# Attention in a fused attention and mixture-of-experts layer: V products cut in two round a maximum product, and the transpose of the maxima placed between the halves

## The chip, the cores and the metric

The kernel runs on one core of one Trainium2 chip. The metric is the device time of one execution, in microseconds (us). Engines named here: PE (TensorE, matrix products; "PEld" is its loading of weights), DVE (VectorE), ACT (ScalarE), POOL (GpSimd) and SP, which issues most DMAs.

## The reference, cut to what matters

Two sequences of 512 tokens with 512 features pass a layer norm, attention with 32 heads of 16 features, a second layer norm and a mixture of 8 experts (2 per token). The change lies in the attention alone:

```python
q, k, v = (proj(w_q), proj(w_k), proj(w_v))            # (2, 32, 512, 16)
scores = jnp.einsum('bhqd,bhkd->bhqk', q, k) / jnp.sqrt(jnp.float32(D_K))
attn = jax.nn.softmax(scores, axis=-1)
out = jnp.einsum('bhqk,bhkd->bhqd', attn, v)
```

## The kernel before, in words

The 64 pairs of sequence and head are worked on in NG = 16 groups of four heads. Softmax needs each query's maximum before the exponentials, and the kernel computes the scores twice. First with queries on the partitions: 16 **maximum products** a group (`key_max`, L759: 48 rows, 128 queries, 512 keys), each followed on DVE by a maximum over its 512 keys (`maximum`, L1466) that ends as one column of neg_max. When all 16 columns of a group are there, PE transposes neg_max (`max_t`, L750), ACT copies the result to max_rows (`maxima`, L1201), and SP sends it by DMA as a 49th row into the stacks q_stack (L486). Then with keys on the partitions: eight **score units** a group of two products each (`scores`, L771), where the 49th row subtracts the maximum; ACT takes the exponential of each unit (L1251) into probs_t. The **V product** (`pv`, L740) multiplies probs_t (128 keys by 512 queries) with v_ones, for four heads at once: each head uses a strip of 32 columns of the array (`tile_position=(0, 32*j)`) and writes 32 partitions of the bank ps_o. Its operands are plain fp32, and each call becomes two matmul records. Four V products, one per 128 keys, make a group; then ACT copies ps_o to o_raw (L1236).

The main loop on PE, `for a, b in steps` (L875 to L904), runs over **quarters**, four to a group. A quarter has four maximum products of the group two ahead (called K0 to K3 here), one V product (V), and two score units (S and S'). Its order before is K0, K1, V, K2, [T], S, K3, S', where T is the transpose of the maxima, in one quarter of four (a % 4 = 1). In the quarters a = 1 to 28 of the loop the number b of the score side is the same as a; after a = 28 one quarter has no maximum products, and from then on b = a + 1. The last quarters, b = 57 and later, have no maximum products either.

Maximum products and transposes take turns in a ring of three PSUM banks (`max_banks`, L361; `turns`, L337 to L343). A turn may start when the reader of the turn three before has finished (`max_bank_free`, L428): DVE's maximum (s_mx), or, where that turn was a transpose, ACT's copy (s_mr). The table of turns and the order of the loop have to agree.

K0 and K2 use rows 0 to 47 of the array, K1 and K3 rows 64 to 111, and the two products of a score unit one half each, so two of these products can be in the array together. All engines execute in the order of the program. ACT's order in a quarter is: the copy o_raw (where b % 4 = 1; it waits for all V products of the group), the copy max_rows (in a transpose quarter), and two exponentials. DVE's is its four maxima, plus a reciprocal (L1529) and a shuffle (L1544) once in two groups.

Of the kernel before, what the change touches and what calls it, by code (L numbers as in the profile page):

```python
# [5 lines left out]
B, S, HID = 2, 512, 512  # L6
# [3 lines left out]
TPB = S // P  # L10
# [6 lines left out]
NG = B * NH // GH  # L17
UNITS = 8
# [27 lines left out]
def moe_layer(nc: bass.Bass, x, wq, wk, wv, wo, gw, w13, w2, w2t, out):  # L46
# [8 lines left out]
    with ctx:  # L55
        def sem(name):
            return ctx.enter_context(nc.semaphore(name))

        def sb(c, name, shape, dt=f32):
            return c.enter_context(nc.sbuf_tensor(name, shape, dt))  # L60
# [41 lines left out]
        q0 = sb(att, "q_stack0", q_shape, f32r)  # L102
# [8 lines left out]
        q1 = sb(att, "q_stack1", q_shape, f32r)  # L111
# [11 lines left out]
        probs_t = sb(att, "probs_t", [P, 2, GH, S])  # L123
# [96 lines left out]
        ps_o = ctx.enter_context(nc.psum_tensor("ps_o", [P, 512], f32))  # L220
# [22 lines left out]
        s_ja = sem("s_ja")  # L243
# [9 lines left out]
        s_ex = sem("s_ex")  # L253
        s_pv = sem("s_pv")
        s_or = sem("s_or")
# [47 lines left out]
        a_count = [n + 1 for n in range(len(jobs))]  # L303
# [20 lines left out]
        def head_at(g, j, rows):  # L324

            at, slot, row = (g // 2) % RING, 2 * (g % 2) + j // 2, HALF * (j % 2)
            return [t[at][row:row + rows, slot, :] for t in (qs, ks)]

        def scores_at(u2):

            pair, par = divmod(u2, 2)
            slot, qt = divmod(pair, TPB)
            return 2 * slot + par, qt, par * 2 * TPB + slot * TPB + qt
# [2 lines left out]

        turns = []  # L337
        for s in range(-2, NG):
            lead = 2 if s < 0 else 7
            turns += [(s + 2, u2) for u2 in range(lead)]  # L340
            turns += [(s + 1, "maxima")] * (s + 1 >= 0)
            turns += [(s + 2, u2) for u2 in range(lead, 4 * TPB)]
        turns = [t for t in turns if t[0] < NG]  # L343

        steps, b = [], 0
# [8 lines left out]
        def group_done(a, b):  # L354

            if a is not None and a % TPB == 1:
                return a // TPB + 1
            return NG - 1 if b == TPB * (NG - 2) + 1 else None
# [66 lines left out]
        def max_bank(g, what):  # L425
            return max_banks[turn_of[g, what] % 3]

        def max_bank_free(eng, g, what):  # L428

            n = turn_of[g, what] - 3  # L430
            if n >= 0:
                before, what = turns[n]
                if what in ("maxima", "projection", "router"):
                    eng.wait_ge({"maxima": s_mr, "projection": s_res, "router": s_t2e}[what], before + 1)
                else:
                    eng.wait_ge(s_mx, before * 16 + what + 1)
# [288 lines left out]
        def _(pe):  # L725
            def three(o, x_hi, x_lo, w_hi, w_lo, start, stop):

                pe.matmul(o, x_hi, w_hi, start=start, stop=False)  # L728
                pe.matmul(o, x_hi, w_lo, start=False, stop=False)  # L729
                return pe.matmul(o, x_lo, w_hi, start=False, stop=stop)  # L730

            def pv(g, kc):

                if not 0 <= g < NG:
                    return
                pe.wait_ge(s_ex, UNITS * g + 2 * (kc + 1))
                if kc == 0 and g >= 1:
                    pe.wait_ge(s_or, g)
                for j in range(GH):
                    last = pe.matmul(ps_o[32 * j:32 * j + 32, :],  # L740
                                     v_ones[:, (g // 8) * TPB + kc, (g % 8) * GH + j, :, :].rearrange("p d o -> p (d o)"),
                                     probs_t[:, kc % 2, j, :], start=(kc == 0), stop=(kc == TPB - 1),
                                     tile_position=(0, 32 * j))
                last.then_inc(s_pv, 1)

            def max_t(g):

                pe.wait_ge(s_mx, 16 * (g + 1))
                max_bank_free(pe, g, "maxima")
                pe.transpose(max_bank(g, "maxima")[0:4 * GH, 0:P], neg_max[:, g % 2, :], ident[:, :]).then_inc(s_mt, 1)  # L750

            def key_max(g, u2):

                if g >= NG:
                    return
                j, qt, _ = scores_at(u2)
                q, k = head_at(g, j, ROWS)
                max_bank_free(pe, g, u2)
                pe.matmul(max_bank(g, u2), q[:, qt * P:(qt + 1) * P], k, start=True, stop=True).then_inc(s_sn, 1)  # L759
# [19 lines left out]
            def opened(o, at, b, i):  # L779

                wide, x2 = (w_hi[0], w_lo[0]), (xnT_hi, xnT_lo)
                pe.wait_ge(s_ja, a_count[n_of[("t", b, TPB - 1)]])
                if i:
                    pe.wait_ge(s_wh, 1)
                else:
                    pe.wait_ge(s_wqh, 1)
                terms = ((0, 0), (0, 1), (1, 0)) if i else ((0, 0), (1, 0), (0, 1))
                for n, (wp, xp) in enumerate(terms):
                    if xp:
                        pe.wait_ge(s_jd, d_count[n_of[("t", b, TPB - 1)]])  # L790
                    elif wp and i:
                        pe.wait_ge(s_wl, 1)
                    elif wp:
                        pe.wait_ge(s_wql, 1)
                    for c in range(HC):
                        last = pe.matmul(o, wide[wp][:, c, at], x2[xp][:, c, :], start=(n == c == 0),  # L796
                                         stop=(n == 2 and c == HC - 1))
                return last

            def v_tail(o, i, c0, c1):  # L800

                at = slice(i * P, (i + 1) * P)
                for c in range(c0, c1):
                    last = three(o, xnT_hi[:, c, at], xnT_lo[:, c, at], w_hi[2][:, c, :], w_lo[2][:, c, :],
                                 c == 0, c == HC - 1)
                return last

            for n, (kind, b, i) in enumerate(jobs[:-1]):
# [10 lines left out]
                if kind == "t":  # L819
                    pe.wait_ge(s_xn, b * TPB + i + 1)  # L820
                    for c in range(HC):
                        last = pe.transpose(o[:, c * P:(c + 1) * P], x_sb[:, b * TPB + i, c * P:(c + 1) * P], ident[:, :])
                else:
# [3 lines left out]
                    if opening:  # L827
                        last = opened(o, at, b, i)
# [3 lines left out]
                    for c in range(0 if opening else HC):  # L832
                        x2 = [t[:, c, :] for t in (xnT_hi, xnT_lo)]
                        w2 = [t[which][:, c, :] for t in (w_hi, w_lo)]
                        if kind == "v":
                            last = three(o, *(t[:, at] for t in x2), *w2, c == 0, c == HC - 1)
                        else:
                            last = three(o, *(t[:, at] for t in w2), *x2, c == 0, c == HC - 1)
# [36 lines left out]
            for a, b in steps:  # L875
                ga, pa = (NG, 0) if a is None else (2 + a // TPB, a % TPB)
                s, p = divmod(b, TPB)
                group, kc = (s - 1, p + 2) if p < 2 else (s, p - 2)
                done = group_done(a, b)
                if ga < NG and pa == 0 and ga % 2 == 0:  # L880
                    pe.wait_ge(s_stack[(ga // 2) % RING], 16 * 12 * (ga // 2 // RING + 1))
                if p == 0 and s < NG:
                    pe.wait_ge(s_row[s % 4], 32 * (s // 4 + 1))

                if b == 0:
                    pe.wait_ge(s_ja, a_count[n_of["v", 1, TPB - 3]])
                    v_tail(ps_o[:, :], TPB - 1, 0, HC // 2)
                key_max(ga, 4 * pa)
                key_max(ga, 4 * pa + 1)
                if b == 0:  # L890
                    pe.wait_ge(s_ja, a_count[n_of["v", 1, TPB - 2]])
                if b == 1:
                    v_tail(ps_o[:, :], TPB - 1, HC // 2, HC).then_inc(s_job, 1)
                if (group, kc) == (0, 0):
                    pe.wait_ge(s_ja, a_count[-1])
                pv(group, kc)
                key_max(ga, 4 * pa + 2)
                if done is not None:
                    max_t(done)
                scores(s, 2 * p)  # L900
                key_max(ga, 4 * pa + 3)
                scores(s, 2 * p + 1)
                if b in FILL:
                    projection(*FILL[b])  # L904
# [70 lines left out]
            for d in range(1, NT):  # L975
                pe.matmul(ps_m[:, d * E:NT * E], ones_b[:, :], pk[:, 0:(NT - d) * E],
                          start=(d == 1), stop=False, skip_group_check=True)
            pe.matmul(ps_m[:, 0:NT * E], before_b[:, :], pk, start=False, stop=True,
                      skip_group_check=True).then_inc(s_rank_0, 1)
            for t in range(NT):  # L980
                last = pe.matmul(ps2[:, 0, 0:E], ones_b[:, :], pk[:, t * E:(t + 1) * E],
                                 start=(t == 0), stop=(t == NT - 1))
# [5 lines left out]
            for t in range(NT):  # L988
                last = pe.matmul(ps4[:, 0, 0:2], row_hot_0[:, t, :], token_of_0[:, t, :],
                                 start=(t == 0), stop=(t == NT - 1))  # L990
# [176 lines left out]
            for half, done in enumerate((s_xt_0, s_xt)):  # L1167
                for c in range(2):
                    at = slice((2 * half + c) * P, (2 * half + c + 1) * P)
                    last = pe.transpose(ps2[:, half, c * P:(c + 1) * P], xg[:, 1, at], ident[:, :])  # L1170
# [696 lines left out]
```

## Time and profile before

| | us |
|---|---|
| median of 3 runs (562.98 to 564.12) | 563.24 |
| the profiled execution | 562.15 |
| its span, which the trace covers | 560.3 |
| PE busy | 537.7 (96%) |
| DVE busy | 386.5 (69%) |
| ACT busy | 324.6 (58%) |

The attention loop takes the stretch from about 95 to 267 us. A busy PE is not PE at its peak: the ends of matmuls are modelled, and of two products in the array together both count. The time at the start of a row is from the start of the span; in brackets stands how long the engine was idle before the row and what released it.

### The profile page before, as it was taken

The page shows a single profiled execution, that of the slowest core. Times are in us where ns is not written, and L with a number is a line of the kernel's source. Part 1 is how long each engine was busy: PE and PEld are TensorE (multiplying, and loading weights), DVE is VectorE, ACT ScalarE, POOL GpSimd, SP SyncE. Part 2 cuts the span into 40 slices and gives each one's busy share as a digit, 9 for nine tenths or more (in the row PEclk, how much of TensorE's full clock was granted, in tenths as well). Part 3 has the DMA queues.
Part 4 walks back from the last instruction along what each step waited for, and adds up shares of the span by engine and source line. Part 5 has one row for each costly group of instructions (what it writes and reads, how often), then busy time and mean ns, then how long its engine had stood idle before and what let it go on. Part 6 is the DMA issues. An engine that isn't in the chain of part 4 may idle for free.

```text
span 560.3 us, 9693 instructions
## 1 busy us (share of the span) xinstructions
PE 537.7 (96%) x3504; PEld 391.4 (70%) x3504; DVE 386.5 (69%) x706; ACT 324.6 (58%) x480; POOL 116.2 (21%) x145
## 2 busy tenths in 40 slices
PE   8999999899999999999999989999999999999991
PEld 6887665333333333333778979999999999999980
DVE  6914657889998999961688986755728375667650
ACT  4322115767878777878345463746657475757540
POOL 3400111002022020622001203234341321241212
PEclk9999999999999999999998999999999999999996
DMA  8390368937465753004464599583764757586112
GB/s 329 103 112 2 56 83 98 114 47 89 70 97 76 92 75 99 12 19 165 156 223 134 185 352 329 145 309 51 287 153 154 267 144 278 117 299 160 32 30 37
DMA packets 29068, 78.19 MB, mean 140 GB/s; under 512 B 7644, under 2 KB 8924, under 8 KB 24538
## 3 DMA queue, kind: packets, MB, share of 16 engines
q1 hardware_dynamic: 23722, 68.84, 47.0%
q0 software_dynamic: 5296, 8.69, 8.4%
q8 instruction: 30, 0.49, 0.4%
q14 instruction: 20, 0.16, 0.1%
HBM read 53.11 MB, written 9.32 MB: 111 GB/s over the span
## 4 chain that ended last, share of the span: by engine, by line
PE 77%; DVE 13%; issue 3%; DMA 2%; ACT 2%; POOL 1%; SPq 0%; POOLq 0%; DVEq 0%; ACTq 0%
PE ps L728 15%; PE ps L729 14%; PE ps L730 14%; PE ps_o L740 8%; DVE neg_max L1466 8%; PE ps L759 6%; PE ps L771 4%; PE ps_m L759 3%; PE ps L796 2%; DVE w_lo L1575 1%; DMA w_sb<-w 1%; PE ps L777 1%; PE ps_o L728 1%; PE ps_m L728 1%; PE ps_m L1022 1%
## 5 line engine op out<-in xcount | busy, mean ns | idle before, releaser
L1251 ACT ACTIVATE probs_t<-ps 128x1024 f32<-128x1024 f32 x128 | 124.2, 1022 | 32.9 <-PE ps L771 32.3
L1466 DVE TENSOR_REDUCE neg_max<-ps 128x1 f32<-128x512 f32 x170 | 111.8, 685 | 14.7 <-PE ps L759 12.1
L728 PE MATMUL ps<-xgT_hi,w_hi 128*128 128x256 f32 (+7 forms) x380 | 109.5, 288 | 1.0 <-DVE xgT_lo L1732 1.0
L729 PE MATMUL ps<-xgT_lo,w_hi 128*128 128x256 f32 (+7 forms) x380 | 108.5, 286 | 0.0
L730 PE MATMUL ps<-xgT_hi,w_lo 128*128 128x256 f32 (+7 forms) x380 | 108.5, 286 | 0.0
L759 PE MATMUL ps<-k_stack,q_stack 48*128 48x512 f32 x170 | 70.3, 456 | 3.8 <-issue 1.7
L728 PEld LDWEIGHTS ps<-xgT_hi,w_hi 128*128 128x128 f32 x380 | 72.0, 189 | 1.3 <-DVE xgT_lo L1732 1.1
L729 PEld LDWEIGHTS ps<-xgT_lo,w_hi 128*128 128x128 f32 x380 | 72.0, 189 | 0.1
L730 PEld LDWEIGHTS ps<-xgT_hi,w_lo 128*128 128x128 f32 x380 | 71.9, 189 | 0.0
L740 PE MATMUL ps_o<-probs_t,v_ones 128*32 128x512 f32 x512 | 68.1, 605 | 0.0
L1749 DVE TENSOR_TENSOR act<-gate,ps 128x256 f32<-128x256 f32 (+7 forms) x48 | 20.7, 430 | 67.8 <-PE ps L730 53.5
L759 PEld LDWEIGHTS ps<-k_stack,q_stack 48*128 48x128 f32 x170 | 28.3, 184 | 52.2 <-DVE neg_max L1466 43.0
L771 PE MATMUL ps<-q_stack,k_stack 49*128 49x512 f32 x256 | 62.1, 430 | 0.4 <-ACT probs_t L1251 0.4
L1466 DVE TENSOR_REDUCE neg_max<-ps_m 128x1 f32<-128x512 f32 x86 | 58.9, 684 | 3.0 <-PE ps_m L759 2.8
L1575 DVE TENSOR_TENSOR w_lo<-w_sb,w_hi 128x1024 fp32r<-128x1024 f32 x48 | 56.5, 1219 | 0.0
L1324 ACT ACTIVATE gate<-ps 128x256 f32<-128x256 f32 (+7 forms) x48 | 18.8, 393 | 61.6 <-PE ps L730 60.4
L1273 ACT ACTIVATE w_hi<-w_sb 128x1024 fp32r<-128x1024 f32 x48 | 48.6, 1056 | 4.2 <-DMA w_sb<-w 4.0
L759 PE MATMUL ps_m<-k_stack,q_stack 48*128 48x512 f32 x86 | 39.3, 457 | 1.0 <-DMA q_stack<-max_rows 0.2
L771 PEld LDWEIGHTS ps<-q_stack,k_stack 49*128 49x128 f32 x256 | 30.1, 185 | 12.3 <-ACT probs_t L1251 7.7
L646 POOL TENSOR_TENSOR q_hi<-q_hi,rec_all 128x512 f32<-128x512 f32 x7 | 9.0, 1284 | 136.1 <-DVE rec_all L1544 136.1
L688 POOL DMA_INDIRECT out<-xn,to_now x20 | 33.8, 1688 | 6.2 <-issue 6.2
L759 PEld LDWEIGHTS ps_m<-k_stack,q_stack 48*128 48x128 f32 x86 | 15.8, 184 | 25.5 <-DVE neg_max L1466 22.5
(329 smaller groups left out, 982.2 us busy)
## 6 DMA issues: line engine op xcount, KB each, us to landing
w_sb<-w SPq DMA_DIRECT2D x16, 1024.0 KB
w_sb<-w SPq DMA_DIRECT2D x8, 1536.0 KB
w_sb<-w SPq DMA_DIRECT2D x8, 1152.0 KB
q_stack<-q_hi SPq DMA_DIRECT2D x32, 128.0 KB, 5.4
k_stack<-k_hi SPq DMA_DIRECT2D x32, 128.0 KB, 5.1
q_stack<-q_lo SPq DMA_DIRECT2D x16, 128.0 KB, 4.7
k_stack<-k_lo SPq DMA_DIRECT2D x16, 128.0 KB, 5.9
q_hi<-o_raw SPq DMA_DIRECT2D x16, 128.0 KB, 4.7
```

What stands on the lines that cost most here:

```text
L688: pool.indirect_dma_start(out=out[:, :], out_offset=bass.IndirectOffsetOnAxis(ap=to_now[0:rows, m:m + 1], axis=0), in_=y_sb[0:rows, m, :], ...
L728: pe.matmul(o, x_hi, w_hi, start=start, stop=False)
L729: pe.matmul(o, x_hi, w_lo, start=False, stop=False)
L730: return pe.matmul(o, x_lo, w_hi, start=False, stop=stop)
L740: last = pe.matmul(ps_o[32 * j:32 * j + 32, :], v_ones[:, (g // 8) * TPB + kc, (g % 8) * GH + j, :, :].rearrange("p d o -> p (d o)"), prob ...
L759: pe.matmul(max_bank(g, u2), q[:, qt * P:(qt + 1) * P], k, start=True, stop=True).then_inc(s_sn, 1)
L771: last = pe.matmul(ps4[:, 2 * (n % 2) + c, :], k[:, kc * P:(kc + 1) * P], q, start=True, stop=True)
L1251: a.activation(probs_t[:, kc % 2, 2 * half:2 * half + 2, :], ps4[:, 2 * (n % 2):2 * (n % 2) + 2, :], ACT.Exp, scale=D ** -0.5).then_inc(s_ ...
L1273: a.activation(w13_hi[:, at], w13_sb[:, at], ACT.Copy).then_inc(s_hi13, 1)
L1466: v.tensor_reduce(neg_max[:, g % 2, col:col + 1], max_bank(g, u2), AX.X, ALU.max, negate=True).then_inc(s_mx, 1)
L1575: v.tensor_tensor(w13_lo[:, at], w13_sb[:, at], w13_hi[:, at].bitcast(f32), ALU.subtract).then_inc(s_lo13, 1)
L1749: v.tensor_tensor(act[:, u % 2, 0:cap], gate[:, u % 2, 0:cap], ps4[:, pair + 1, 0:cap], ALU.mult).then_inc(s_act, 1)
```

## The change

1. V is issued in two halves: queries 0 to 255 (V1), and 256 to 511 (V2). Each half is again four strips, with the weights loaded anew, and 256 columns in place of 512. The semaphore s_pv is raised after V2.
2. K1 stands between V1 and V2. K0 is now the last product ahead of V1.
3. In a transpose quarter T stands between K1 and V2, where before it followed K2. The table of turns gives it the place behind K1: the number of turns ahead of it is 6 and no longer 7 (group 2 keeps 7, since its first quarters keep their old order).

The quarters b = 0 and 1, and those without maximum products, are as before. That leaves the 54 quarters a = 2 to 55.

```diff
-            lead = 2 if s < 0 else 7
+            lead = 2 if s < 0 else 7 if s == 0 else 6
@@
-            def pv(g, kc):
+            def pv(g, kc, q0, q1):
...
-                pe.wait_ge(s_ex, UNITS * g + 2 * (kc + 1))
-                if kc == 0 and g >= 1:
-                    pe.wait_ge(s_or, g)
+                if q0 == 0:
+                    pe.wait_ge(s_ex, UNITS * g + 2 * (kc + 1))
+                    if kc == 0 and g >= 1:
+                        pe.wait_ge(s_or, g)
                 for j in range(GH):
-                    last = pe.matmul(ps_o[32 * j:32 * j + 32, :],
+                    last = pe.matmul(ps_o[32 * j:32 * j + 32, q0:q1],
...
-                                     probs_t[:, kc % 2, j, :], start=(kc == 0), stop=(kc == TPB - 1),
-                                     tile_position=(0, 32 * j))
-                last.then_inc(s_pv, 1)
+                                     probs_t[:, kc % 2, j, q0:q1], start=(kc == q0 == 0), stop=(kc == TPB - 1 and q1 == S),
+                                     tile_position=(0, 32 * j), skip_group_check=True)
+                if q1 == S:
+                    last.then_inc(s_pv, 1)
@@
                 key_max(ga, 4 * pa)
-                key_max(ga, 4 * pa + 1)
...
-                pv(group, kc)
+                elif ga < NG:
+                    if (group, kc) == (0, 0):
+                        pe.wait_ge(s_ja, a_count[-1])
+                    pv(group, kc, 0, S // 2)
+                    key_max(ga, 4 * pa + 1)
+                    if done is not None:
+                        max_t(done)
+                    pv(group, kc, S // 2, S)
+                else:
+                    pv(group, kc, 0, S)
                 key_max(ga, 4 * pa + 2)
-                if done is not None:
+                if done is not None and (ga == NG or b < 2):
                     max_t(done)
```

PE's order in an ordinary quarter before, from K0 and K1 (the row with x2) through V, K2, S, K3 to S'; ps and ps_m are banks of the ring where the operands are k_stack,q_stack, and the two banks of a score unit where they are q_stack,k_stack:

```order
L759 MATMUL ps<-k_stack,q_stack 128x512 [waits s_mx] x2
L740 MATMUL ps_o<-probs_t,v_ones 32x512 [waits s_ex]
L740 MATMUL ps_o<-probs_t,v_ones 32x512 x3
L759 MATMUL ps_m<-k_stack,q_stack 128x512 [waits s_mx]
L771 MATMUL ps<-q_stack,k_stack 128x512 [waits s_ex]
L771 MATMUL ps<-q_stack,k_stack 128x512
L759 MATMUL ps<-k_stack,q_stack 128x512 [waits s_mx]
L771 MATMUL ps<-q_stack,k_stack 128x512 [waits s_ex]
L771 MATMUL ps<-q_stack,k_stack 128x512
```

The same quarter in the changed kernel, from K0 through V1, K1, V2, K2, S, K3 to S' (pv is now L741, key_max L761, scores L773):

```order
L761 MATMUL ps<-k_stack,q_stack 128x512 [waits s_mx]
L741 MATMUL ps_o<-probs_t,v_ones 32x256 [waits s_ex]
L741 MATMUL ps_o<-probs_t,v_ones 32x256 x3
L761 MATMUL ps_m<-k_stack,q_stack 128x512 [waits s_mx]
L741 MATMUL ps_o<-probs_t,v_ones 32x256 x4
L761 MATMUL ps<-k_stack,q_stack 128x512 [waits s_mx]
L773 MATMUL ps<-q_stack,k_stack 128x512 [waits s_ex]
L773 MATMUL ps<-q_stack,k_stack 128x512
L761 MATMUL ps<-k_stack,q_stack 128x512 [waits s_mx]
L773 MATMUL ps<-q_stack,k_stack 128x512 [waits s_ex]
L773 MATMUL ps<-q_stack,k_stack 128x512
```

The wide V is now two half V, and K1 has moved from ahead of it to between them. On PE, a transpose quarter before, from K2 through T (L750), S, K3 and S' to the next quarter's K0 and K1 and the start of its V:

```order
L759 MATMUL ps_m<-k_stack,q_stack 128x512 [waits s_mx]
L750 MATMUL ps<-ident,neg_max 16x128 [waits s_mx]
L771 MATMUL ps<-q_stack,k_stack 128x512 [waits s_ex]
L771 MATMUL ps<-q_stack,k_stack 128x512
L759 MATMUL ps<-k_stack,q_stack 128x512 [waits s_mx]
L771 MATMUL ps<-q_stack,k_stack 128x512 [waits s_ex]
L771 MATMUL ps<-q_stack,k_stack 128x512
L759 MATMUL ps_m<-k_stack,q_stack 128x512 [waits s_mx]
L759 MATMUL ps<-k_stack,q_stack 128x512 [waits s_mr]
L740 MATMUL ps_o<-probs_t,v_ones 32x512 [waits s_or,s_ex]
```

The same quarter in the changed kernel, from K1 through T (now L752), V2, K2, S, K3 and S' to the next quarter's K0 and the start of its V1:

```order
L761 MATMUL ps<-k_stack,q_stack 128x512 [waits s_mx]
L752 MATMUL ps_m<-ident,neg_max 16x128 [waits s_mx]
L741 MATMUL ps_o<-probs_t,v_ones 32x256 x4
L761 MATMUL ps<-k_stack,q_stack 128x512 [waits s_mx]
L773 MATMUL ps<-q_stack,k_stack 128x512 [waits s_ex]
L773 MATMUL ps<-q_stack,k_stack 128x512
L761 MATMUL ps<-k_stack,q_stack 128x512 [waits s_mx]
L773 MATMUL ps<-q_stack,k_stack 128x512 [waits s_ex]
L773 MATMUL ps<-q_stack,k_stack 128x512
L761 MATMUL ps_m<-k_stack,q_stack 128x512 [waits s_mr]
L741 MATMUL ps_o<-probs_t,v_ones 32x256 [waits s_or,s_ex]
```

The wait for s_mr, ACT's copy of the transposed maxima, has moved from the next quarter's K1 to its K0. The orders of ACT and DVE are unchanged.

## Rows read from the trace of the kernel before

**Rows 1.** The page: busy time by engine, and the granted clock by slice

```profile
PE 537.7 (96%) x3504; PEld 391.4 (70%) x3504; DVE 386.5 (69%) x706; ACT 324.6 (58%) x480; POOL 116.2 (21%) x145
...
PEclk9999999999999999999998999999999999999996
```

**Rows 2.** The page, groups: busy us, mean ns of one, idle before, releaser

```profile
L1466 DVE TENSOR_REDUCE neg_max<-ps 128x1 f32<-128x512 f32 x170 | 111.8, 685 | 14.7 <-PE ps L759 12.1
...
L740 PE MATMUL ps_o<-probs_t,v_ones 128*32 128x512 f32 x512 | 68.1, 605 | 0.0
```

**Rows 3.** Waits from 113 to 244 us: total us, times, longest

```profile
PEld ps L759 <- DVE neg_max L1466: 36.5, 54, 0.8
...
PEld ps_m L759 <- DVE neg_max L1466: 17.6, 26, 0.8
```

**Rows 4.** Timeline of an ordinary quarter: start us, us, what

```profile
143.24 1.06 PE L740 MATMUL ps_o<-probs_t,v_ones 128*32 128x512 f32 x8
143.28 1.28 DVE L1466 TENSOR_REDUCE neg_max<-ps 128x1 f32<-128x512 f32 x2
...
144.23 0.18 PEld L759 LDWEIGHTS ps_m<-k_stack,q_stack 48*128 48x128 f32 x1 [0.84 <-DVE neg_max L1466]
...
144.76 0.69 DVE L1466 TENSOR_REDUCE neg_max<-ps_m 128x1 f32<-128x512 f32 x1 [0.21 <-PE ps_m L759]
...
145.04 0.40 PE L759 MATMUL ps<-k_stack,q_stack 48*128 48x512 f32 x1
145.07 1.94 ACT L1251 ACTIVATE probs_t<-ps 128x1024 f32<-128x1024 f32 x2 [0.75 <-PE ps L771]
...
145.51 0.18 PEld L759 LDWEIGHTS ps_m<-k_stack,q_stack 48*128 48x128 f32 x1 [0.51 <-DVE neg_max L1466]
...
145.94 1.07 PE L740 MATMUL ps_o<-probs_t,v_ones 128*32 128x512 f32 x8
```

**Rows 5.** Timeline of the transpose quarter with the copy o_raw

```profile
137.78 1.06 PE L740 MATMUL ps_o<-probs_t,v_ones 128*32 128x512 f32 x8
...
138.78 0.50 PE L759 MATMUL ps_m<-k_stack,q_stack 48*128 48x512 f32 x1
138.91 0.60 ACT L1236 ACTIVATE o_raw<-ps_o 128x512 f32<-128x512 f32 x1
...
139.21 0.28 PE L750 MATMUL ps<-ident,neg_max 128*16 128x128 f32 x1
...
139.41 0.50 PE L771 MATMUL ps<-q_stack,k_stack 49*128 49x512 f32 x2
139.52 0.27 ACT L1201 ACTIVATE max_rows<-ps 16x128 fp32r<-16x128 f32 x1
...
140.22 0.40 PE L759 MATMUL ps<-k_stack,q_stack 48*128 48x512 f32 x1
...
140.54 1.06 PE L740 MATMUL ps_o<-probs_t,v_ones 128*32 128x512 f32 x8
```

**Rows 6.** Timeline of the quarter with DVE's shuffle

```profile
132.05 1.07 PE L740 MATMUL ps_o<-probs_t,v_ones 128*32 128x512 f32 x8
...
132.09 0.74 DVE L1544 STREAM_SHUFFLE rec_all<-rec_row 128x512 f32<-128x512 f32 x1
...
134.65 0.18 PEld L759 LDWEIGHTS ps<-k_stack,q_stack 48*128 48x128 f32 x1 [0.35 <-DVE neg_max L1466]
...
135.08 1.07 PE L740 MATMUL ps_o<-probs_t,v_ones 128*32 128x512 f32 x8
```

**Rows 7.** Timeline at the long gap of PE before b = 8

```profile
112.59 0.46 PE L759 MATMUL ps<-k_stack,q_stack 48*128 48x512 f32 x1 [1.73 <-issue]
```

**Rows 8.** Timeline round b = 29, the quarter without maximum products

```profile
168.00 1.06 PE L740 MATMUL ps_o<-probs_t,v_ones 128*32 128x512 f32 x8
...
169.91 1.07 PE L740 MATMUL ps_o<-probs_t,v_ones 128*32 128x512 f32 x8
...
172.17 0.40 PE L759 MATMUL ps<-k_stack,q_stack 48*128 48x512 f32 x2
```

More of the change, by code:

```diff
@@ L888, in _ @@
                 key_max(ga, 4 * pa)
-                key_max(ga, 4 * pa + 1)
                 if b == 0:
+                    key_max(ga, 4 * pa + 1)
                     pe.wait_ge(s_ja, a_count[n_of["v", 1, TPB - 2]])
-                if b == 1:
+                elif b == 1:
+                    key_max(ga, 4 * pa + 1)
                     v_tail(ps_o[:, :], TPB - 1, HC // 2, HC).then_inc(s_job, 1)
-                if (group, kc) == (0, 0):
-                    pe.wait_ge(s_ja, a_count[-1])
-                pv(group, kc)
+                elif ga < NG:
+                    if (group, kc) == (0, 0):
+                        pe.wait_ge(s_ja, a_count[-1])
+                    pv(group, kc, 0, S // 2)
+                    key_max(ga, 4 * pa + 1)
+                    if done is not None:
[3 more added lines that the diff above has]
+                    pv(group, kc, 0, S)
                 key_max(ga, 4 * pa + 2)
-                if done is not None:
+                if done is not None and (ga == NG or b < 2):
                     max_t(done)
```

## The prediction

> **What bounds the kernel now.** I read the page first: PE is busy for 96% of the span, and at full clock in the slices of the attention loop [rows 1]. In the groups DVE's maxima take 685 ns each and have idle time before them that PE releases, while the V product's records have none [rows 2]. So neither engine alone explains the loop. The waits say what PE's weight loads stand for: DVE's maxima, 80 times between 113 and 244 us [rows 3]. Then the timeline of one quarter [rows 4], which shows a ring. With V's start as 0 (143.24):
> - K2 starts at 0.99, when V is through (144.23).
> - DVE begins K2's maximum at 1.52 (144.76), after 0.21 idle, and it takes 0.69.
> - K1 of the next quarter needs that bank. It starts at 2.27 (145.51), its weights after 0.51 of waiting.
> - The next V starts at 2.70 (145.94).
>
> The sum is 0.99 + 0.53 + 0.75 + 0.43 = 2.70 us. DVE alone would need 4 × 0.60 = 2.40 (two maxima in a row take 1.28, so the second begins 0.60 after the first), and ACT's two exponentials take 1.94. A quarter is bound by this ring, not by an engine's work.
>
> **What the ordinary quarter becomes.** K1 no longer stands between K2's maximum and V, so the ring is cut. What is left is PE's own chain, worked out from V1's start backwards and forwards with rows 4:
> - K2's start to K0's start: 145.04 − 144.23 = 0.81, unchanged.
> - K0 to V1. K0's weights are loaded under another product (duration 0.40, against 0.49 or 0.50 with the load showing). The nearest row is the product at 140.22, also 0.40, after which V starts at 140.54 [rows 5]: 0.32 to 0.33.
> - V1. The whole V takes 0.99. It has two sets of four records; the second set begins 1.06 − 0.59 = 0.47 after the first (0.59 is its records' length, as 605 is the mean of both sets), so 0.45 to 0.47 for 512 columns, and 0.52 to 0.54 for the second set with what follows it until K2. At full clock two cycles a column make 0.43, which leaves 0.03 and 0.11 that do not depend on columns. A half is 0.24 + 0.33 = 0.57. If all of the 0.99 scaled, it would be 0.50; if a quarter of it were fixed, 0.62.
> - K1 alone, its load showing: 145.51 to 145.94, 0.43.
> - V2: 0.57 once more.
>
> Sum: 0.81 + 0.33 + 0.57 + 0.43 + 0.57 = 2.71, against 2.70. The wait on DVE is gone, and the second set-up of V plus the second change between K1 and V has taken its place. I take no change: 0.00 ± 0.05 a quarter. With the ends 0.50 and 0.62 for a half it would be −0.14 to +0.10; the row nearest to a half is V itself, so I stay in the middle.
>
> The Trainium skill bears on this twice. "TensorEngine Tiling (Array Packing)", section Key Properties, says that changing the tiling mode drains TensorE; the trace agrees, with 0.33 from K0 to V for a product whose 512 columns are 0.21 at full clock. "TensorE: Matmul & The Clock Gate", section Step-by-step, says that weight loads are pulled ahead of running matmuls if row groups differ or they go to the background buffer. By that one K1's and V2's loads would be hidden; the load at 145.51 and K2's at 144.23 stand bare. The last rival is what that rule would do here.
>
> Is anything else late? With V1 as 0, DVE begins K1's maximum at 1.20, K2's at 2.10, K3's at 2.70, and K0's at 3.30, which is 0.60 in the next quarter. K0's load at 2.15 needs K1's maximum (1.20 + 0.69 = 1.89): 0.2 of room, the least there is. ACT's exponentials begin 0.84 after K2 (145.07 − 144.23), at 2.41, and end at about 4.3, thus 1.6 in the next quarter, before S' asks for them at 1.9.
>
> **The transpose quarter.** Before it took 2.76 (137.78 to 140.54). T costs little there, since it lies in DVE's slack. Now T stands in PE's own chain: K1 to T is 0.43 (138.78 to 139.21), T to what follows 0.20 (139.21 to 139.41), in place of K1 to V2's 0.43. The quarter is 2.71 + 0.20 = 2.90 or 2.91, +0.14.
>
> In the transpose quarters up to b = 28 a wait comes on top. ACT first copies o_raw, which needs V2, and only then max_rows, and the next K0 now waits for that copy. Before, o_raw started 1.13 after V (138.91), which is 0.14 after its end, and max_rows was ready at 139.79, 2.01 after V: early for a K1 at 2.27. Now V2 ends at 0.57 + 0.43 + 0.20 + 0.57 = 1.77; o_raw from 1.90, max_rows from 2.51 to 2.78 (steps of 0.61 and 0.27 [rows 5]), K0 at about 2.82 in place of 2.35. K0 is the last thing before V1, load showing, so V1 comes at 2.82 + 0.43 = 3.25: +0.49. It holds up PE and nothing else: DVE has K3 until 3.5, and ACT's exponentials slip by 0.15.
>
> After b = 28 o_raw falls in the quarter before, so T's copy is done by 1.9 and only the 0.14 stays. Its row of maxima goes out by DMA and is wanted two quarters later; T is now earlier in its quarter by 0.4, which covers it.
>
> **Shuffle quarters.** 132.05 to 135.08 is 3.03: the shuffle (0.74, 0.63 in effect) delays K1 to 134.65 [rows 6]. In the new order all of DVE's maxima begin 0.57 later against V1, and K0, which needs the maximum before the one K1 needed (0.60 earlier), waits to about 2.63: V1 at 3.06, +0.03. No gain there.
>
> **The ends.** Each run of changed quarters ends with one that had its K1 ahead of V for nothing more. From V to the next V was 1.91 (168.00 to 169.91 [rows 8]). Now K1 and V2 lie in it: 0.57 + 0.43 + 0.57 + 0.91 = 2.48, +0.57, at b = 28 and again at b = 56. The gains of 0.57 at the runs' beginnings don't pay: at b = 2 it runs into PE's gap of 1.73 before 112.59 [rows 7], where K0 waits for a row of maxima behind the loads of the stacks, and at b = 30 K0 and K1 went into the array together (172.17) and K0 alone takes as long. For the same reason all that the quarters up to b = 7 gain or lose is swallowed; the row of maxima may leave 0.2 later, I count +0.1.
>
> **Sum.** Five transpose quarters (b = 9, 13, 17, 21, 25; the one at 5 is swallowed) × 0.49 = 2.4. Seven after b = 28 × 0.14 = 1.0. Five shuffle quarters × 0.03 = 0.2. Two ends × 0.57 = 1.1. The gap 0.1. Ordinary quarters 0.0. Together +4.8. Nothing behind the loop waits for a clock time, so it goes through: 562.15 + 4.8 = 567.0 for a profiled execution, and as the median shown is 1.09 above the profiled one, 563.24 + 4.8 = 568.0.
>
> **The rivals.** Changed quarters that count, without the two ends: 20 + 26 = 46.
> - *The copy doesn't hold up K0, or a free DVE makes it good.* For it: DVE has 0.3 idle a quarter to catch up with. Against: K0 is followed by V1 on PE, with no DVE in between. +4.8 − 5 × 0.35 = +3.1: 566.3.
> - *A half costs more than 0.57.* Each half has its own eight records and loads; at 0.62, 46 × 0.10 = 4.6 more, 572.6. Against: the records of a V start 7 ns apart or so, far below a set's 0.24.
> - *The halves or the changes cost less, and it comes out level.* At 0.10 a quarter less (K1's bare load hidden, 0.49 against 0.40), −4.6 + 4.8: 563.4.
> - *Not slower: loads are hidden on both sides of K1.* Then K1 costs 0.23 and V1 0.47 without its drain: 0.81 + 0.33 + 0.47 + 0.23 + 0.57 = 2.41, just at DVE's 2.40. 46 × −0.29 + 4.8 = −8.5: 554.7. It decides for faster from about 2.58 a quarter (4.8 / 46 = 0.10, and 0.02 for the margin). Against: each such load in rows 4 stands bare after V.
> - *The change doesn't do what it says*: the wait on K2's maximum could stay where K1 is. By the sum it is 0.4 or more early, so I give it no case of its own.
>
> **Chances.** The forecast 0.50 (its own range 565 to 570.5, from ± 0.05 in 46 quarters), the hidden copy 0.10, the dearer half 0.10, level 0.15, faster 0.15. About 0.2% (1.1 us) is what a measurement of this kernel can tell. Slower takes the first three, 0.70. The range 560.5 to 572.5 leaves out the larger part of the last case and the upper half of the dearer half.
>
> **What would show it.** Ordinary quarters of 2.70 from V1 to V1, with no wait of K1's load on DVE; V1 to K1 0.57; 3.25 in the transpose quarters up to b = 25, with K0's load released by ACT's max_rows; 2.90 in those from b = 30; PE's records 54 × 8 more, 3936. A quarter of 2.60 or less would make it wrong, as would a quarter that holds DVE's maxima back to back.

## The result, and the profile after

| | before | changed |
|---|---|---|
| median, us | 563.11 (4 runs, 562.75 to 564.12) | 607.33 (4 runs, 605.49 to 621.88) |
| profiled execution, us | 562.15 | 607.44 |
| its span | 560.3 | 605.7 |
| mean granted clock of TensorE | 0.989 | 0.909 |

The changed kernel takes 1.077 times as long (95% interval 1.074 to 1.080), 44 us more where I had forecast 4.8. The ratio leaves out one run of 621.88, in which the clock was lower still (0.878).

The page of the changed kernel, where rows 1 and 2 were read before:

```profile
PE 585.0 (97%) x3936; PEld 414.9 (68%) x3936; DVE 389.4 (64%) x706; ACT 323.1 (53%) x480; POOL 118.1 (20%) x145
...
PEclk8999999855555589999999999999999999999997
...
L1476 DVE TENSOR_REDUCE neg_max<-ps 128x1 f32<-128x512 f32 x171 | 113.4, 686 | 42.0 <-PE ps L761 40.7
```

PE's records are the 3936 that were expected, DVE's maxima take as long as before [rows 2], but they now wait 42 us for PE. The line of the clock says why: six slices in a row at 5, which is half of full speed. The stretches (length, then busy time and records of PE, PEld, DVE, ACT and POOL, the granted clock, DMA) give its borders:

```profile
100.00:112.00 12.00, 12.00 (x108) 5.18 (x106) 10.81 (x18) 9.24 (x12) 0.00 (x0) 1.00 1.04 117
112.00:114.00 2.00, 1.36 (x14) 0.49 (x6) 1.77 (x4) 1.23 (x2) 0.00 (x0) 1.00 0.59 61
114.00:116.00 2.00, 1.63 (x14) 0.68 (x18) 1.01 (x3) 1.16 (x2) 0.00 (x0) 1.00 0.04 8
116.00:118.00 2.00, 2.00 (x15) 0.97 (x7) 1.65 (x3) 0.58 (x1) 0.00 (x0) 0.66 0.00 0
118.00:214.00 96.00, 96.00 (x485) 37.12 (x484) 54.64 (x87) 42.00 (x51) 6.31 (x6) 0.50 0.38 50
214.00:216.00 2.00, 2.00 (x12) 0.33 (x12) 0.71 (x2) 1.85 (x2) 0.00 (x0) 0.59 0.00 0
...
218.00:290.00 72.00, 72.00 (x630) 31.41 (x629) 65.99 (x112) 54.20 (x65) 16.72 (x17) 1.00 0.37 64
```

From about 116.7 to 215.6 us TensorE ran at 1.2 in place of 2.4 GHz. PE counts as busy for all of the 96 us from 118 to 214, and still did not get its full clock back. The clock fell some two microseconds behind PE's gap ahead of b = 8, and it came back in the quarter b = 29, which has no maximum products. The timeline of the changed kernel there, against [rows 7]:

```profile
114.34 0.18 PEld L761 LDWEIGHTS ps<-k_stack,q_stack 48*128 48x128 f32 x1 [1.43 <-issue]
114.37 0.47 PE L761 MATMUL ps<-k_stack,q_stack 48*128 48x512 f32 x1 [1.02 <-issue]
...
114.77 0.64 PE L741 MATMUL ps_o<-probs_t,v_ones 128*32 128x256 f32 x8
...
118.09 1.08 PE L741 MATMUL ps_o<-probs_t,v_ones 128*32 128x256 f32 x8
```

The gap was even shorter than before (1.02 against 1.73 of idle PE), and before the clock had held. A half V takes 0.64 in the records at 114.77, at full clock, and 1.08 from 118.09 on. An ordinary quarter at half clock, in the same trace:

```profile
151.95 1.08 PE L741 MATMUL ps_o<-probs_t,v_ones 128*32 128x256 f32 x8
...
152.96 0.79 PE L761 MATMUL ps<-k_stack,q_stack 48*128 48x512 f32 x1
153.68 1.08 PE L741 MATMUL ps_o<-probs_t,v_ones 128*32 128x256 f32 x8
153.79 0.69 DVE L1476 TENSOR_REDUCE neg_max<-ps 128x1 f32<-128x512 f32 x1 [0.97 <-PE ps L761]
154.69 0.29 PEld L761 LDWEIGHTS ps<-k_stack,q_stack 48*128 48x128 f32 x1 [0.81 <-DVE neg_max L1476]
...
156.69 1.08 PE L741 MATMUL ps_o<-probs_t,v_ones 128*32 128x256 f32 x8
```

V1 to V1 is 4.74, and DVE waits in every quarter (0.97 here). And one at full clock, from the second run of quarters (b = 30 on), where the clock held; these rows answer to [rows 4]:

```profile
242.05 0.64 PE L741 MATMUL ps_o<-probs_t,v_ones 128*32 128x256 f32 x8
242.62 0.50 PE L761 MATMUL ps<-k_stack,q_stack 48*128 48x512 f32 x1
243.05 0.64 PE L741 MATMUL ps_o<-probs_t,v_ones 128*32 128x256 f32 x8
243.62 0.49 PE L761 MATMUL ps_m<-k_stack,q_stack 48*128 48x512 f32 x1
...
244.42 0.40 PE L761 MATMUL ps<-k_stack,q_stack 48*128 48x512 f32 x1
...
244.75 0.64 PE L741 MATMUL ps_o<-probs_t,v_ones 128*32 128x256 f32 x8
```

Here the sum of the prediction can be checked step by step: V1 0.57, K1 0.43, V2 0.57, K2 to K0 0.80, K0 to V1 0.33, in all 2.70 as before.

Where the 45.3 us between the two profiled executions come from, by the starts of V: up to b = 8 1.8 (113.01 against 114.77; 1.6 of it is there before the first changed quarter, in the maximum products at 86.74 and 88.37); from b = 8 to b = 29 42.5 (56.90 against 99.40, the stretch at half clock); from b = 30 to b = 57 1.7 (73.75 against 75.42). That is 46.0; what follows the loop took some 0.6 less.

### The profile page after: what moved, and what is told of

It reads as the page before. It is cut to its first block, busy times and chain, and to the rows that moved or that the text cites. A ratio compares the mean times of both kernels' runs of the same rounds, so it can differ in the third digit from the quotient of the medians.

```text
span 605.7 us, 10557 instructions
## 1 busy us (share of the span) xinstructions
PE 585.0 (97%) x3936; PEld 414.9 (68%) x3936; DVE 389.4 (64%) x706; ACT 323.1 (53%) x480; POOL 118.1 (20%) x145
## 4 chain that ended last, share of the span: by engine, by line
PE 86%; DVE 6%; DMA 2%; issue 2%; ACT 1%; POOL 1%; SPq 0%; POOLq 0%; DVEq 0%; ACTq 0%
PE ps_o L741 14%; PE ps L728 14%; PE ps L729 13%; PE ps L730 13%; PE ps L761 9%; PE ps L773 6%; PE ps_m L761 4%; PE ps L798 1%; DVE w_lo L1585 1%; DMA w_sb<-w 1%; DVE neg_max L1476 1%; PE ps_o L728 1%; PE ps_m L728 1%; PE ps_m L730 1%; PE ps_o L729 1%
## 5 line engine op out<-in xcount | busy, mean ns | idle before, releaser
L1476 DVE TENSOR_REDUCE neg_max<-ps 128x1 f32<-128x512 f32 x171 | 113.4, 686 | 42.0 <-PE ps L761 40.7
L741 PE MATMUL ps_o<-probs_t,v_ones 128*32 128x256 f32 (+1 forms) x944 | 98.0, 495 | 0.0
L761 PE MATMUL ps<-k_stack,q_stack 48*128 48x512 f32 x171 | 85.9, 536 | 1.6 <-issue 1.0
L773 PE MATMUL ps<-q_stack,k_stack 49*128 49x512 f32 x256 | 75.4, 504 | 0.0
L761 PEld LDWEIGHTS ps<-k_stack,q_stack 48*128 48x128 f32 x171 | 35.5, 222 | 50.5 <-DVE neg_max L1476 35.5
L741 PEld LDWEIGHTS ps_o<-probs_t,v_ones 128*32 128x32 f32 x944 | 20.3, 118 | 44.3 <-issue 42.5
L761 PE MATMUL ps_m<-k_stack,q_stack 48*128 48x512 f32 x85 | 45.9, 539 | 0.1
L773 PEld LDWEIGHTS ps<-q_stack,k_stack 49*128 49x128 f32 x256 | 36.9, 228 | 9.9 <-ACT probs_t L1261 6.8
L761 PEld LDWEIGHTS ps_m<-k_stack,q_stack 48*128 48x128 f32 x85 | 19.1, 225 | 23.5 <-DVE neg_max L1476 16.6
```

The source lines that it names most:

```text
L741: last = pe.matmul(ps_o[32 * j:32 * j + 32, q0:q1], v_ones[:, (g // 8) * TPB + kc, (g % 8) * GH + j, :, :].rearrange("p d o -> p (d o)"), ...
L773: last = pe.matmul(ps4[:, 2 * (n % 2) + c, :], k[:, kc * P:(kc + 1) * P], q, start=True, stop=True)
L1476: v.tensor_reduce(neg_max[:, g % 2, col:col + 1], max_bank(g, u2), AX.X, ALU.max, negate=True).then_inc(s_mx, 1)
```

## The experiments

My theory after the result (theory A): the idle gap ahead of b = 8 takes the clock down, and the changed quarters, unlike the old ones, don't bring it back up. Rivals: changed quarters lose the clock by themselves (B); no order of this loop gets a lost clock back (C); and of the change's three parts, any one could be what matters.

**e1, halves adjacent.** V stays in two halves, K1 and T go back.

```diff
-            lead = 2 if s < 0 else 7 if s == 0 else 6
+            lead = 2 if s < 0 else 7
@@
-                    pv(group, kc, 0, S // 2)
                     key_max(ga, 4 * pa + 1)
-                    if done is not None:
-                        max_t(done)
+                    pv(group, kc, 0, S // 2)
                     pv(group, kc, S // 2, S)
@@
-                if done is not None and (ga == NG or b < 2):
+                if done is not None:
                     max_t(done)
```

> The changed kernel with K1 back ahead of V and T back behind K2 (ring of turns as before); V stays cut in two halves, which now follow each other. Theory A1, the halves themselves take TensorE's clock down after the gap of b = 7: half clock from about 116 to 217 us again, time over 600 us. Theory A2, it is the lone K1 between the halves (one product in the array where there were two, and two more changes between K and V): full clock throughout, and the ring of the old order with a V of 1.03 to 1.06 in place of 0.99, so 2.74 to 2.77 a quarter and 565 to 567 us.

Measured: 565.82 us (562.17 to 567.53), against 566.67 (562.53 to 572.24) for the kernel before on the same chip; ratio 1.000 (0.994 to 1.006). Neither theory had it right: in the profiled run (567.33) the clock fell here too, but came back. The stretches of e1:

```profile
114.00:116.00 2.00, 2.00 (x20) 1.00 (x22) 1.29 (x2) 0.00 (x0) 0.00 (x0) 0.63 0.03 8
116.00:126.00 10.00, 10.00 (x57) 4.79 (x53) 6.02 (x10) 5.12 (x7) 0.00 (x0) 0.50 0.12 29
...
128.00:130.00 2.00, 1.92 (x16) 0.86 (x8) 1.12 (x2) 0.82 (x1) 0.00 (x0) 0.96 1.10 116
```

Some 14 us at half clock, then full again. Its ordinary quarters at full clock are 2.70 (149.46 to 152.15 in its trace), and the two halves take 1.00 together (149.46 to 150.46): cutting V in two costs nothing while the halves follow each other. So the halves by themselves don't hold the clock down; what is left is K1 between them, or T.

**e2, the transpose back behind K2.** K1 stays between the halves.

```diff
-            lead = 2 if s < 0 else 7 if s == 0 else 6
+            lead = 2 if s < 0 else 7
@@
                     key_max(ga, 4 * pa + 1)
-                    if done is not None:
-                        max_t(done)
                     pv(group, kc, S // 2, S)
@@
-                if done is not None and (ga == NG or b < 2):
+                if done is not None:
                     max_t(done)
```

> The changed kernel with the transpose T back behind K2 and its turn back to place 7; the halves with K1 between them stay. If T's place took the clock down: full clock, transpose quarters of about 3.2 us (T stands alone in PE's chain behind K2), 566 to 570 us. If the halves with K1 between them did it: half clock from about 116 to 217 us again, 600 to 610 us.

Measured: 611.80, 571.24, 570.42 and 613.31 us, with mean clocks of 0.907, 0.987, 0.991 and 0.905. Each expectation came true in two runs, those at full clock just above the 566 to 570 that I had named. In the profiled one (611.80) the clock was at half from 114.8 to 217.2 us, as in the changed kernel. So the clock stays down without T between the halves, and with e1 it is K1's place that decides. Whether T's place makes the fall more frequent (four runs of four against two of four), so few runs can't tell. The time of 570 to 571 is the price at full clock: T behind K2 makes a transpose quarter of 3.28, where T between the halves makes 2.91. Placing T there, taken alone, was the better place for the cut V.

**e3 and e4, rows first.** SP sends half of the loads of the stacks behind the row of maxima that PE waits for ahead of b = 8; e3 in the changed kernel, e4 in the kernel before.

```diff
                 elif s == 0:
                     ready(3)
-                    stack(3, range(2), "qk")
+                    stack(3, range(1), "qk")
+                elif s == 1:
+                    stack(3, [1], "qk")
```

> The changed kernel, but SP issues the second half of the fourth pair's stack loads one turn later, behind the row of maxima of group 2, which PE waits for ahead of b = 8. Theory A, the gap and the split quarters together take the clock down: without the gap the clock stays at full all through, and the time is what my sum gives without a gap to swallow the first quarters, 565 to 568 us. Theory B, split quarters lose the clock by themselves sooner or later: it falls elsewhere, 590 us and more.

> The kernel before with the same later issue of half the stack loads. The gap of 1.43 us over an ordinary quarter (PE from 110.9 to 112.6) goes: about 561.8 us at full clock, 1.4 less than before. If the row of maxima is late for another reason than the loads ahead of it, no change.

Measured: e3 564.69 us (564.50 to 566.05), e4 559.96 (559.61 to 560.97). Both are below what I had named (565 to 568, and about 561.8). Theory B falls: without the gap the changed kernel kept its full clock in the profiled run and, by the mean clocks of 0.990 to 0.994, in the three others. The line of the clock of e3:

```profile
PEclk9999999999999999999999999999999999999997
```

The timeline of e4 where the gap was, from V of b = 7 to V of b = 8:

```profile
109.00 1.07 PE L742 MATMUL ps_o<-probs_t,v_ones 128*32 128x512 f32 x8
...
111.69 0.64 PE L742 MATMUL ps_o<-probs_t,v_ones 128*32 128x512 f32 x4
```

2.69 in place of 4.13. The difference of e3 and e4, 4.7 us on the same chip, is what the change costs at full clock with no gap in the way. And e4 is faster than the kernel before, which ran at 562.53 to 572.24 beside it: ratio 0.991 (0.987 to 0.995). The spread of that kernel is itself a trace of the same thing, if theory A holds.

**e5, a long gap in the kernel before.** POOL makes PE wait ahead of b = 8.

```diff
+            pool.wait_ge(s_pv, 6)
+            for n in range(24):
+                pool.memset(idle_s[:, :], 0.0).then_inc(s_gap, 1)
+                pool.wait_ge(s_gap, n + 1)
@@
             for a, b in steps:
...
+                if b == 8:
+                    pe.wait_ge(s_gap, 24)
```

> The kernel before with a long gap of PE ahead of b = 8: PE waits there for a chain of 24 small memsets on POOL that begins when V of b = 7 is done, some 5 to 8 us. Theory A, the old order gets the full clock back by itself and the split order does not: half clock for less than 20 us after the gap, quarters of 4 to 4.5 us in it, then 2.70 again; in all the gap plus 5 to 10 us, 572 to 580 us. Theory C, no order of the loop gets it back before the quarter without maximum products: half clock for about 100 us, over 600 us.

Measured: 573.28 and 573.08 us. From V of b = 7 to V of b = 8 it took 7.10 us. The stretches of e5:

```profile
110.00:116.00 6.00, 2.40 (x15) 0.83 (x15) 3.08 (x5) 3.49 (x4) 3.19 (x21) 1.00 0.58 61
...
118.00:134.00 16.00, 16.00 (x63) 6.18 (x56) 9.23 (x15) 6.69 (x9) 0.00 (x0) 0.50 0.32 45
...
138.00:180.00 42.00, 41.23 (x249) 15.82 (x253) 39.49 (x67) 33.11 (x40) 6.35 (x6) 1.00 0.57 78
```

Half clock from 115.9 to 136.4 us, ordinary quarters of 4.16 in it, then 2.70 again. The old order gets its clock back in the fifth quarter behind the gap; theory C falls. One of its quarters at half clock (V, K2, K0 with K1, V):

```profile
130.81 1.93 PE L746 MATMUL ps_o<-probs_t,v_ones 128*32 128x512 f32 x8
132.67 0.79 PE L765 MATMUL ps<-k_stack,q_stack 48*128 48x512 f32 x1
...
134.12 0.92 PE L765 MATMUL ps<-k_stack,q_stack 48*128 48x512 f32 x2
134.97 1.76 PE L746 MATMUL ps_o<-probs_t,v_ones 128*32 128x512 f32 x8
```

It is the ring of [rows 4] at half clock. V takes 1.86 (0.99 before); K2's maximum begins 0.83 after K2 (0.53), K1 follows it 0.74 later (0.75), and V 0.73 after K1 (0.43): 4.16. DVE's part has not grown, and K0 and K1 start almost together, at 134.12 and 134.24.

**e6, K1 behind the whole V.** With the loads of e4; V is not cut.

```diff
-                key_max(ga, 4 * pa + 1)
+                if b < 2:
+                    key_max(ga, 4 * pa + 1)
@@
                 pv(group, kc)
+                if b >= 2:
+                    key_max(ga, 4 * pa + 1)
                 key_max(ga, 4 * pa + 2)
```

> The kernel before with the stack loads behind the row of maxima (so no gap ahead of b = 8), and K1 moved behind the whole V, to go into the array together with K2. V is not cut. If the wait of K1 on K2's maximum is what a quarter is worth, this takes it away without a second set-up of V, and the quarter should fall towards DVE's 2.40: 545 to 550 us. By the ring of three banks it only turns into another wait: K0 now needs K1's maximum, 0.53 + 0.73 + 0.43 + 1.00 = 2.69 a quarter, the time of the kernel with rows first, 560 us, or 1 more from the ends of the runs.

Measured: 568.19 us (567.72 to 569.59), ratio 1.008 (1.004 to 1.011) to the kernel before; full clock in the loop. The timeline of e6, one quarter:

```profile
144.25 1.07 PE L742 MATMUL ps_o<-probs_t,v_ones 128*32 128x512 f32 x8
...
145.25 0.18 PEld L761 LDWEIGHTS ps_m<-k_stack,q_stack 48*128 48x128 f32 x1
...
145.78 0.69 DVE L1471 TENSOR_REDUCE neg_max<-ps 128x1 f32<-128x512 f32 x1 [0.23 <-PE ps_m L761]
...
146.62 0.47 PE L761 MATMUL ps<-k_stack,q_stack 48*128 48x512 f32 x1 [0.18 <-DVE neg_max L1471]
...
147.03 1.06 PE L742 MATMUL ps_o<-probs_t,v_ones 128*32 128x512 f32 x8
```

The wait of PE on DVE has moved from K1 to K0, and the quarters are 2.70 to 2.77. The ring of three banks is confirmed: taking one product out of it puts the next one in. The total is 7 us above what I expected. The 13 transpose quarters are enough for it: they took 3.30 in place of 2.77 or so in e4, as T there is in the ring too.

**e7 and e8, the gap filled.** Twelve spare bf16 products of 256 columns in the gap ahead of b = 8; e7 in the changed kernel, e8 in the kernel before.

```diff
+                if b == 8:
+                    max_bank_free(pe, ga, 0)
+                    keep_warm(max_bank(ga, 0), 12)
                 if ga < NG and pa == 0 and ga % 2 == 0:
```

> The changed kernel with 12 spare bf16 products of 256 columns on PE in the gap ahead of b = 8, into the bank that K0 is about to use; loads and order are untouched, so the gap stays as long, but PE is not idle in it. Theory A, the idle gap takes the clock down and the split order keeps it there: full clock, 566 to 569 us (my prediction's sum). If it is the time lost there for another reason, or split quarters as such: 600 us and more, or a part of the runs.

> The kernel before with the same 12 spare products in the gap ahead of b = 8. By theory A the runs of the kernel before at 566 and 572 us had lost the clock for some us there, so this holds 562.5 to 563.5 in every run. Otherwise its runs spread like those of the kernel before.

Measured: e7 567.84 us in eight runs (566.38 to 568.58), ratio 1.007 (1.004 to 1.010); e8 562.04 in ten runs (561.18 to 564.34), ratio 0.998 (0.995 to 1.001). The kernel before, in 20 runs beside them: 561.30 to 573.52, six of them above 565. The timeline of e7 in the gap:

```profile
111.79 0.40 PE L773 MATMUL ps<-q_stack,k_stack 49*128 49x512 f32 x2
112.12 1.49 PE L779 MATMUL ps<-idle_b 128*128 128x256 bf16 x12
113.54 0.50 PE L761 MATMUL ps<-k_stack,q_stack 48*128 48x512 f32 x1
113.97 0.64 PE L741 MATMUL ps_o<-probs_t,v_ones 128*32 128x256 f32 x8
```

PE waits for the same row of maxima, but is not idle meanwhile, and the clock stays at full through all 98 us from 118 to 216. This is the sharpest test: 1.5 us of products without use save 40 us. The changed kernel itself was not run on the chip of e7, but e9 and e10 below ran on one chip together: with the spare products ahead of b = 8 the clock held there (e9), without them it fell (e10). In e8 no run is above 565 us, though it spreads by 3 us where I expected 1; with ten runs against six of 20, that can still be chance.

**e9, a long gap at another place.** e7 with e5's chain ahead of b = 40.

```diff
+                if c == 3:
+                    pool.wait_ge(s_pv, 38)
+                    for n in range(24):
+                        pool.memset(idle_s[:, :], 0.0).then_inc(s_gap, 1)
+                        pool.wait_ge(s_gap, n + 1)
                 pool.wait_ge(s_sh, c + 1)
@@
+                if b == 40:
+                    pe.wait_ge(s_gap, 24)
```

> The changed kernel with the 12 spare products ahead of b = 8 (full clock there, 567.8 us) and a long gap of PE ahead of b = 40, a chain of 24 small memsets on POOL that begins when V2 of b = 39 is done, 4.5 us over V's start to start. Theory A (split quarters don't get the full clock back, wherever it was lost): half clock from the gap to the end of the quarters with maximum products at b = 56, about 17 quarters of 4.74, so 17 x 2.04 = 35 us and the gap: 605 to 612 us. If what holds the clock down has to do with b = 8 to 28 (the stack loads, the first run): back at full clock within 20 us, as the kernel before after its long gap, 575 to 582 us.

Measured: 605.58 us (605.27 to 608.16). Stretches of e9:

```profile
200.00:210.00 10.00, 5.77 (x48) 2.38 (x40) 5.42 (x10) 4.08 (x6) 5.47 (x26) 0.83 0.58 79
...
214.00:250.00 36.00, 36.00 (x187) 13.65 (x179) 20.55 (x33) 16.10 (x19) 1.68 (x2) 0.50 0.13 39
...
290.00:300.00 10.00, 10.00 (x55) 3.67 (x57) 1.22 (x3) 7.74 (x10) 0.15 (x1) 0.90 0.32 94
```

Half clock from 206.7 to 292.0 us, to the end of the quarters with maximum products (V of b = 57 is at 290.33). So a long gap does it at b = 40 too, far from the stack loads ahead of b = 8; from V1 of b = 39 to V1 of b = 40 it took 7.47 us. Whether a gap of 1 us would be enough there was not tried.

**e10, a burst in the low stretch.** The changed kernel with its gap, and 24 spare products ahead of b = 12 (the edit of e7 with `b == 12` and 24).

> The changed kernel, its gap ahead of b = 8 as it is, and 24 spare bf16 products of 256 columns ahead of K0 of b = 12, four quarters later (2.6 us at full clock, 5.1 at half). Theory A: the clock falls at 116 us and comes back with the burst or behind it, and the split quarters then keep it: 575 to 585 us in runs that lose it, 569 to 571 in runs that don't. If split quarters can't hold a clock that was once lost, or the burst is too short: half clock to b = 29 as before, 605 to 612 us.

Measured: 578.25, 576.19, 577.64 and 568.38 us, mean clocks 0.975, 0.978, 0.975 and 0.993. Stretches of e10:

```profile
114.00:118.00 4.00, 4.00 (x24) 1.69 (x24) 1.79 (x3) 0.45 (x1) 0.00 (x0) 0.54 0.01 4
118.00:130.00 12.00, 12.00 (x61) 4.39 (x59) 6.89 (x11) 6.56 (x8) 0.00 (x0) 0.50 0.28 45
...
134.00:138.00 4.00, 4.00 (x34) 2.49 (x36) 0.69 (x1) 0.58 (x1) 0.00 (x0) 0.90 0.00 0
...
142.00:240.00 98.00, 97.59 (x837) 41.59 (x833) 88.05 (x150) 73.65 (x88) 13.18 (x13) 1.00 0.57 83
```

The clock fell at 114.3, came back at 134.8 with the burst, and the changed quarters then kept it. The fourth run, by its mean clock of 0.993, did not lose it, although the kernel with its gap is the same.

## Why the prediction was wrong

**The step that failed** is the term "Ordinary quarters 0.0" in the sum, and under it the sentence of the first paragraph that PE is "at full clock in the slices of the attention loop". I took the clock of the profile before as given and worked all lengths out from rows at full clock. In the 20 quarters b = 9 to 28, of the 46 that I counted, ordinary ones took 4.74 in place of 2.70 and transpose quarters 5.06 where I had 3.25; from b = 8 to b = 29 that made 42.5 us, and no rival of mine had the clock in it. I had the gap ahead of b = 8 in [rows 7] and used it as something that swallows time. It was the place at which the clock was at stake: 0.8 to 1.9 us of idle PE (0.83 in e2, 1.02 in the changed kernel, 1.73 before, 1.91 in e1), which the old quarters survived or recovered from (the runs of the kernel before beside e1, up to 572.24 us, and e5), and the new ones did not (e2, e9, e10).

**The price at full clock was right, within half a microsecond.** e7 has the changed kernel's order and loads and keeps its clock: 567.84, 5.0 above the kernel before beside it, against the 568.0 and 4.8 of the prediction. Part of that match is luck. From V of b = 8 to V of b = 57 e7 took 137.46 against 133.24 in the profile before, 4.2 more where my terms for that stretch make 4.7; another 1.0 was already there at b = 8, where I had counted 0.1. e3 minus e4 is 4.7 too, but with no gap to swallow anything and a sixth quarter with o_raw, so it is not the same sum. The terms, from the changed kernel's second run of quarters and from e7:

| term | predicted | measured |
|---|---|---|
| half V | 0.57 | 0.57 |
| ordinary quarter | 2.71 | 2.70 |
| transpose quarter with o_raw | 3.25 | 3.13 |
| transpose quarter after b = 28 | 2.90 | 2.91 |
| shuffle quarter | 3.06 | 3.05 |
| quarter b = 28 | 2.48 | 2.48 |

The copy does hold up K0, as the timeline of e7 shows (its rows begin with the V1 of b = 9, and K0 is released by ACT):

```profile
116.67 0.64 PE L741 MATMUL ps_o<-probs_t,v_ones 128*32 128x256 f32 x8
...
118.58 0.60 ACT L1249 ACTIVATE o_raw<-ps_o 128x512 f32<-128x512 f32 x1 [0.27 <-PE ps_o L741]
...
119.37 0.18 PEld L761 LDWEIGHTS ps<-k_stack,q_stack 48*128 48x128 f32 x1 [0.40 <-ACT max_rows L1214]
...
119.80 0.64 PE L741 MATMUL ps_o<-probs_t,v_ones 128*32 128x256 f32 x8
```

K0 came at 2.70 after V1, where I had 2.82: o_raw began as predicted, and the two copies together took 0.1 less than I had added up. Five such quarters at 3.13 make up the half microsecond. The gap swallowed the first quarters as I said: in the changed kernel it ended 1.78 later than before, of which 1.63 lie ahead of all changed quarters, so 0.15 where I counted 0.1.

**The rivals.** The rule of "TensorE: Matmul & The Clock Gate" in the Trainium skill, section Step-by-step, that loads are pulled ahead where row groups don't conflict or the background buffer takes them, did not come true for K1 and V2: in e7 K1's load stands bare at 117.24, with 0.41 of idle PEld before it, and V2's at 120.80, with 0.24. The draining between modes that "TensorEngine Tiling (Array Packing)" in the Trainium skill, section Key Properties, tells of fits what the halves pay twice: 0.57 each, where a whole V takes 0.99. The rule that I should have weighed, of "TensorE: Matmul & The Clock Gate" in the Trainium skill, stands in the section What's actually happening: the low clock is the default state, and activity releases it. The runs agree that idle time brings it down: with the gap filled the clock held (e7), with it idle it fell. They don't agree that a busy PE is enough to bring it back: 96.00 of 96 us counted as busy in the records, and the clock stayed at half.

**What stays open.** By e1 and e2 it is K1 alone between the halves that keeps the clock down, together with the changes of mode round it. At half clock K0 and K1 of the old order start 0.12 apart, and the quarter takes 4.16 for the same products, against 4.74; PE counts as busy without a break in both (16.00 of 16 us in e5, 96.00 of 96 in the changed kernel). Why the one regains the clock and the other does not, no run varied by itself, and it stays open. Nor is it shown why a gap of about 1 us (1.02, 0.83 and 1.08 in the three traces) took the clock down in all four runs of the changed kernel, in two of four of e2 and in three of four of e10, while the 1.73 of the profile before did not. When the clock fell is known from one trace of each kernel; for the other runs only the mean clock speaks.

## What to carry to other kernels

When a change rearranges TensorE's work and leaves its chain as long as before, ask what it does to the clock: look for the idle gaps of PE in the trace, even of 1 us, and ask whether the new order could climb back from 1.2 GHz after one. A kernel whose runs spread by 1 or 2% with differing mean clocks may be near that edge already, as the kernel before here (561.30 us at 0.994, 573.52 at 0.964). Spare products in the gap (e7), or better a transfer moved out of the way of the one that PE waits for (e4, 559.96 us, the lowest median here), kept the clock in every run here. And in a ring of few banks, a wait removed at one product returns at the next (e6); count the ring again before cutting anything in two.

## What the runs showed of the hardware that I had not expected

- TensorE stayed at 1.2 GHz for 99 us with PE busy in all of it by the records, and came back within one quarter of another mix of work (b = 29; V there begins at 214.17, and the full clock at 215.6).
- Two half V products one after the other take as long as one whole (1.00 in e1, against 0.99): there the second loading of the strips' weights costs nothing that shows. With one product of another mode between them the halves take 0.57 each, 1.14 in place of 1.00, and K1 another 0.43.
- At half clock the old quarter takes 4.16, 1.54 times its 2.70: 0.75 of its ring is DVE's maximum and what goes with it, which is still 0.74. The changed one takes 4.74, 1.76 times (V1 1.01, K1 0.72, V2 1.01, K2 to V1 2.00), since all its steps are PE's. A chain that lies on PE alone is the more exposed to the clock.
